# Expert jobs in pairs on TensorE, attention added by GpSimd, and a block closed without GpSimd's drain

## What is computed

```python
def _L0_attn_ref(x, W_off, b_off, W_attn, b_attn, W_out, b_out):
    off = (x @ W_off + b_off).reshape(Bx, Nx, H, P, 2)
    w = softmax((x @ W_attn + b_attn).reshape(Bx, Nx, H, P), axis=-1)
    idx = ...                                   # from off[..., 0], clipped to 0..127
    g = take_along_axis(x[:, 0, :], idx, axis=1)
    s = sum(g * w, axis=(2, 3))                 # one number per token
    return broadcast_to(s[..., None], (Bx, Nx, C)) @ W_out + b_out

def _ffn(x, w1, w2, w3):
    return silu(x @ w1.T) * (x @ w3.T) @ w2.T   # 128 -> 256 -> 128
# two shared experts for every token, and of 8 routed experts the best two per token,
# weighted by a softmax over their two logits
x = x + attn(xn) + ffn(xn)
```

## Time and profile before

| | |
|---|---|
| timed runs, median (range) | 418.75 us (418.43 to 419.17) |
| span of the profiled execution, first to last instruction | 416.8 us |
| busy: TensorE / VectorE / ScalarE / GpSimd | 366.9 (88%) / 331.8 (80%) / 190.5 (46%) / 189.7 (46%) us |
| mean granted TensorE clock | 0.985 of full speed |
| chain of work that ended last, by engine | PE 74%, DVE 13%, ACT 6%, DMA 2% |
| expert stage | 224.1 to 405.6 us |
| the shared experts' last sum ends | 224.95 us |
| the sums of the last job end | 406.46 us |

### The profile page before, as it was taken

One profiled execution on the slowest core, in us unless ns is written; L12 is line 12 of the kernel. 1 busy time (PEld: TensorE's weight loads), 2 busy tenths in 40 slices (PEclk: granted clock), 3 DMA queues, 4 the chain that ended last, 5 costly groups with the idle time before them and its releaser, 6 DMA issues.

```text
span 416.8 us, 12515 instructions
## 1 busy us (share of the span) xinstructions
PE 366.9 (88%) x4333; PEld 316.9 (76%) x4333; DVE 331.8 (80%) x929; ACT 190.5 (46%) x446; POOL 189.7 (46%) x152
## 2 busy tenths in 40 slices
PE   0157797789999999999999999999999999999990
PEld 0155564467677777777779999999999999999990
DVE  5988989987967699999996998886666666666760
ACT  2778728395322466666666344422222222222220
POOL 0434500404777776343200000001888888888863
PEclk9988999999999999999999999999999999999997
DMA  8944620000117199988873345554565956654332
GB/s 298 296 97 104 126 77 0 2 0 16 48 56 167 57 187 179 182 166 165 168 110 60 75 132 159 131 133 118 67 63 67 79 62 66 65 65 39 35 34 19
DMA packets 98871, 41.36 MB, mean 99 GB/s; under 512 B 73600, under 2 KB 92416, under 8 KB 98816
## 3 DMA queue, kind: packets, MB, share of 16 engines
q1 hardware_dynamic: 87120, 31.82, 36.7%
q0 software_dynamic: 11264, 8.69, 16.0%
q10 hardware_dynamic: 432, 0.11, 0.1%
HBM read 10.94 MB, written 12.88 MB: 57 GB/s over the span
## 4 chain that ended last, share of the span: by engine, by line
PE 74%; DVE 13%; ACT 6%; DMA 2%; issue 1%; POOL 1%; POOLq 0%; DVEq 0%; ACTq 0%
PE pY L832 18%; PE pY L655 11%; PE pAB L806 8%; PE pAB L804 8%; PE pAB L805 8%; PE pAB L643 5%; PE pAB L645 5%; PE pAB L644 5%; PE pV L667 4%; ACT units L870 3%; DVE hbuf L1189 2%; ACT wsp L941 2%; PE pV L621 2%; DVE hot L1095 1%; DMA xT<-hot 1%
## 5 line engine op out<-in xcount | busy, mean ns | idle before, releaser
L1065 POOL DMA_INDIRECT out_dram<-xT,rows x64 | 99.1, 1549 | 104.6 <-DMA out_dram<-base 83.3
L1011 ACT ACTIVATE units<-pAB 128x512 f32<-128x512 f32 x78 | 46.5, 596 | 119.6 <-PE pAB L806 119.6
L1053 POOL DMA_INDIRECT sorted_rows<-rows,slot x64 | 67.2, 1050 | 59.0 <-issue 32.3
L805 PE MATMUL pAB<-rows,wsp 128*128 128x128 f16 x512 | 89.0, 219 | 0.0
L806 PE MATMUL pAB<-rows,wsp 128*128 128x128 f16 x512 | 89.0, 219 | 0.0
L804 PE MATMUL pAB<-rows,wsp 128*128 128x128 f16 x512 | 89.0, 219 | 0.0
L832 PE MATMUL pY<-wsp,hbuf 128*128 (+1 forms) x620 | 86.4, 282 | 0.3 <-issue 0.3
L1476 DVE SCALAR_TENSOR_TENSOR hbuf<-pAB,units 128x512 f32<-128x512 f32 x78 | 53.6, 687 | 31.7 <-PE pAB L806 29.3
L832 PEld LDWEIGHTS pY<-wsp,hbuf 128*128 128x128 f32 x620 | 75.6, 192 | 0.8 <-issue 0.5
L655 PE MATMUL pY<-wsp,hbuf 128*128 128x128 f32 x512 | 70.2, 280 | 0.0
L655 PEld LDWEIGHTS pY<-wsp,hbuf 128*128 128x128 f32 x512 | 64.3, 192 | 4.1
(11 more groups left out here) (164 smaller groups left out, 586.1 us busy)
## 6 DMA issues: line engine op xcount, KB each, us to landing
base<-in_x SPq DMA_DIRECT2D x8, 512.0 KB, 7.5
out_dram<-base SPq DMA_DIRECT2D x16, 256.0 KB, 2.4
wraw<-in_wall SPq DMA_DIRECT2D x10, 256.0 KB, 2.8
rows<-hot SPq DMA_DIRECT2D x8, 256.0 KB, 2.7
proj<-sorted_rows SPq DMA_DIRECT2D x27, 68.5 KB, 1.9
wsp<-in_wall SPq DMA_DIRECT2D x10, 128.0 KB
sorted_rows<-rows,slot POOLq DMA_INDIRECT x64, 2.4
out_dram<-xT,rows POOLq DMA_INDIRECT x64, 3.4
```

The lines of the kernel that those rows point to most:

```text
L805: pe.matmul(o, hi, x(1), start=False, stop=False)
L1053: pool.indirect_dma_start(sorted_rows, bass.IndirectOffsetOnAxis(ap=slot[:, t:t + 1].bitcast(U32), axis=0), rows[:, t, :], None, bounds_ch ...
L1065: pool.indirect_dma_start(out_rows, bass.IndirectOffsetOnAxis(ap=meta[:, t, DEST - CW:DEST - CW + 1].bitcast(U32), axis=0), yt[:, t], None ...
```

## The change

1. `EXTRA_FROM` is 4: extras at places 4 to 17.
2. TensorE runs over pairs of jobs: turn of pair s, F of pair s-1, S of pair s-2, so F F S S instead of F S. The expert numbers are read five tiles ahead instead of three. VectorE makes its sums in pairs too, behind the product of the second job (`two_sums`).
3. The attention is added by GpSimd (`add_attention`), per block of four tiles a product into `attn_part` and a sum into `base`, before it waits for the writes and sends. SyncE writes block i once F(i) is done, from turn 8 on.
4. The side table is made at units 22 (VectorE), 25 (TensorE and ScalarE); `extra_table` behind unit 23. `sides` has a tile of its own, which `wp_raw` and `ident32` share.
5. The block is made with `no_gpsimd_drain=True`: GpSimd has no drain ahead of the closing barrier.

```diff
-SPREAD_UNIT = UNITS - 4
+SPREAD_UNIT, SIDES_UNIT = 22, 25
-ADDS = 3
-EXTRA_FROM = 8
+EXTRA_FROM = 4
...
-WRITE_AT = [min(n for n in range(AHEAD, STEPS) if FIRST_OF_TURN[n - AHEAD + 1] >= TPB * (i + 1) // ADDS + 5) for i in range(NB)]
+WRITE_AT = [min(n for n in range(AHEAD, STEPS) if LAST_OF_TURN[n - AHEAD] >= i) for i in range(NB)]
...
+        sides16 = sb("sides16", [P, TILES * 2 * E], F16)
+        wp_raw = sides16[:, 2 * P:2 * P + 2 * PROJ].bitcast(F32)
+        ident32 = sides16[:, 0:2 * P].bitcast(F32)
+        sides = sides16[:].rearrange("p (t k e) -> p t k e", k=2, e=E)
+        attn_part = aw_row[:, 0:2 * BLK].rearrange("p (r j c) -> p r j c", r=2, j=TPB)
...
-        block = ctx.enter_context(nc.Block())
+        block = ctx.enter_context(nc.Block(no_gpsimd_drain=True))
...
+                if n == SIDES_UNIT:
+                    pe.wait_ge(table_ready, 1)
+                    pe.wait_ge(spread_ready, 1)
+                    for b in range(2):
+                        mm = pe.matmul(pV[:, b, :], c["ones"][:], spread.rearrange("p t m -> p (t m)")[:, b * BLK:(b + 1) * BLK],
+                                       start=True, stop=True)
+                    mm.then_inc(sides_done, 1)
...
-                if q == 1:
-                    spread_sides()
...
-            pipeline(pe, NJOB, UNROLL, NJOB // UNROLL, [(0, r_turn), (SECOND, r_second), (FIRST, r_first)])
+            def of_pair(part):
+                def both_jobs(g, r):
+                    for q in (2 * (UNROLL * g + r), 2 * (UNROLL * g + r) + 1):
+                        part(q // UNROLL, q % UNROLL)
+                return both_jobs
+            pipeline(pe, NJOB // 2, UNROLL, NJOB // 2 // UNROLL, [(0, of_pair(r_turn)), (1, of_pair(r_first)), (2, of_pair(r_second))])
...
+            def add_attention():
+                for i in range(NB + 1):
+                    if i < NB:
+                        if i == 0:
+                            pool.wait_ge(attn_saved, APAIRS)
+                            pool.wait_ge(y_read, NB)
+                        if i >= 2:
+                            pool.wait_ge(attn_added, i - 1)
+                        nc.gpsimd.tensor_tensor(attn_part[:, i % 2], csum[:].unsqueeze(1).broadcast_to([P, TPB, P]),
+                                                attn_all[:, TPB * i:TPB * (i + 1)].unsqueeze(2).broadcast_to([P, TPB, P]),
+                                                ALU.mult).then_inc(attn_scaled, 1)
+                    if i:
+                        pool.wait_ge(attn_scaled, i)
+                        row = base[:, TPB * (i - 1):TPB * i, :]
+                        nc.gpsimd.tensor_tensor(row, row, attn_part[:, (i - 1) % 2], ALU.add).then_inc(attn_added, 1)
+            add_attention()
             pool.wait_ge(out_done, 16 * NB)
...
-            pipeline(dve, NJOB, UNROLL, NJOB // UNROLL, [(4, side_sums), (4, y_first), (4, y_second), (2, r_hf), (3, side_products),
-                                                         (3, r_attention), (4, load_tiles), (2, extra_shares)])
+            def two_sums(g, r):
+                if r % 2:
+                    for part in (side_sums, y_first, y_second):
+                        part(g, r - 1)
+                    for part in (side_sums, y_first, y_second):
+                        part(g, r)
+            pipeline(dve, NJOB, UNROLL, NJOB // UNROLL, [(2, r_hf), (4, two_sums), (3, side_products),
+                                                         (4, load_tiles), (2, extra_shares)])
```

More of the change, by code:

```diff
@@ L620, in routing_products @@
                     for a in range(NPAIR):
-                        mm = pe.matmul(pV[:, 1, 256:256 + NT], ident32[:], place[:, a, :], start=(a == 0), stop=(a == NPAIR - 1))
+                        mm = pe.matmul(pV[:, 1, 256:256 + NT], ident32, place[:, a, :], start=(a == 0), stop=(a == NPAIR - 1))
                     mm.then_inc(place_done, 1)
@@ L747, in first_addresses @@
                 elif u < 4:
-                    for k in range(2):
-                        ready_expert(u - 1, k)
+                    for t in {1: (0, 1), 2: (2, 3), 3: (4,)}[u]:
+                        for k in range(2):
+                            ready_expert(t, k)
                 else:
@@ L755, in _ @@
             straight(UNITS - ROUND, UNITS, both + [(0, first_addresses, UNITS - ROUND, UNITS)])
[L756 to L763, removed]
             def r_turn(g, r):
@@ L1412, in routed_low @@
                     split_low(g - (ATT - 1), u // 4)
-            while unit[0] < ROUND * ATT - 8:
-                shared_unit()
-            assert unit[0] == ROUND * ATT - 8
-            for n in range(8):
-                shared_unit()
-                one_hot(ATT - 1 + (n + 4) // ROUND, (n + 4) % ROUND)
-                if n >= 6:
-                    weighted_high(ATT - 1, n)
             def extra_table():
@@ L1434, in extra_table, with spread_out @@
                 v.scalar_tensor_tensor(active[:], f(0), 0.0, f(1), ALU.is_gt, ALU.mult).then_inc(extras_ready, 1)
-            def spread_out(g, u):
-                if ROUND * g + u == SPREAD_UNIT:
-                    for r in range(TURNS):
-                        dve.wait_ge(hot_turned[r], 16 * (BATCH - 1))
-                    v.tensor_tensor(spread, c["ident"][:, 0:TILES].unsqueeze(2).broadcast_to([P, TILES, 2 * E]),
-                                    tab_f[:, 2:2 + 2 * E].unsqueeze(1).broadcast_to([P, TILES, 2 * E]),
-                                    ALU.mult).then_inc(spread_ready, 1)
+            def spread_out():
+                dve.wait_ge(table_done, 1)
+                v.tensor_tensor(spread, c["ident"][:, 0:TILES].unsqueeze(2).broadcast_to([P, TILES, 2 * E]),
+                                tab_f[:, 2:2 + 2 * E].unsqueeze(1).broadcast_to([P, TILES, 2 * E]),
+                                ALU.mult).then_inc(spread_ready, 1)
+            while unit[0] < SPREAD_UNIT:
+                shared_unit()
+            spread_out()
+            while unit[0] < ROUND * ATT - 8:
+                shared_unit()
+            extra_table()
+            assert unit[0] == ROUND * ATT - 8
+            for n in range(8):
+                shared_unit()
+                one_hot(ATT - 1 + (n + 4) // ROUND, (n + 4) % ROUND)
+                if n >= 6:
+                    weighted_high(ATT - 1, n)
             start, end = ROUND * ATT, UNITS
@@ L1450, in _ @@
             rounds(dve, ATT + 1, UNITS // ROUND - 1, both)
[L1451 removed]
+            straight(UNITS - ROUND, UNITS + 4, both)
             extra_tile = {}
```

41 lines of the change are left out of this document (12 added, 29 removed).

## The result

| | before | changed |
|---|---|---|
| median of the runs timed together | 418.90 us (418.43 to 419.17, 4 runs) | 415.81 us (414.32 to 416.09, 4 runs) |
| ratio, 95% interval | | 0.992 (0.990 to 0.994) |
| profiled execution, span | 416.8 us | 412.5 us (the one of 414.32) |
| granted TensorE clock | 0.985 | 0.976 |
| GpSimd busy | 189.7 us | 225.3 us |

(The 418.75 ahead is the median of three of these four runs.) The change is faster by 3.1 us. In the two profiled executions it is 4.3. The changed kernel's executions differ among themselves: the four runs have spans of 412.5, 413.5, 413.9 and 414.3, and the profile is of the shortest. What a longer run has that this one hasn't is the main question of the experiments.

What follows compares the result with a forecast made beforehand. TensorE was taken to bound the expert stage, with a serial end of sums, sends and close. -0.3 (pairs, nearly eaten at the end) and -4.1 (no drain) made -4.4 us: span 412.4, median 414.4 us, range 413.2 to 418.8.

Steps and rivals of the forecast that it cites:

- the forecast's own case: The prediction's main case for the whole kernel: 414.4 us, bounds 413.4 to 415.6, chance 58%.
- the 416.6 of two rivals: GpSimd's attention slower than taken, or VectorE mildly delayed by the port (12%); or no gain from pairs on TensorE (5%).
- No drain, -4.1: Close of the block: without GpSimd's drain the wait after the last send shrinks, -4.1 us, bounds 4.4 saved and 0.
- The rival that the drain hides nothing: Close of the block: the 4.5 us wait is the barrier's or DMA queue's own; 418.5 us, chance 15%.
- Pairs on TensorE, -2.2: Expert stage: 39 fewer entries from first products (F) to float32 second products (S), 0.0557 us each, -2.2 us.
- +0.3 for S(76): Last jobs on TensorE: job 76's second products wait for the sums of job 74, +0.3 us, bounds 0.1 to 0.6.
- The end, "-0.3 in all": Last sends on GpSimd: four in a row nearly eat the pairs' gain, leaving -0.3 us, bounds -0.5 and +0.5.
- Side table, 0: Shared experts: the moved table delays VectorE's unit 24 product to about 119.4, hidden from TensorE; 0, bounds 0 and +0.5.
- Attention on GpSimd, 0: Expert stage: 2.35 us per block on an idle GpSimd, sixteen blocks to about 265; VectorE not the bound, 0.
- neither rival of it: VectorE waits for GpSimd at the shared SBUF port: severe 420.5 us, 8%; mild 416.6, 12% together with slower GpSimd.
- writes and loads, "5 us spare: 0": SyncE's queue: the last extra lands by 251.5, TensorE wants it at 256.5, so no cost.
- the distance of 1.95: Gap from the profiled span 416.8 to the median 418.75, kept to turn the predicted span 412.4 into 414.4 us.

Runs made afterwards that it cites:

- the execution that stalled: Profiled execution of the changed kernel run once more with nothing edited; span 413.4 us, median of its runs 415.16 us, ratio 0.9921 to the kernel before.

## Why the prediction held, and where it was off

**Direction and range** held: 415.81 lies in 413.2 to 418.8. The forecast of 414.4 was 1.4 too low, and the time lies just above the 413.4 to 415.6 given for the forecast's own case, nearer to the 416.6 of two rivals. The time alone would not tell these cases apart; the traces and the edits do.

**No drain, -4.1.** Right in mechanism and 0.3 too small: alone it is 4.4 in one group and 4.0 in another, 4.45 and 4.35 by the spans, and the wait at the close went from 4.5 to 0.2. The rival that the drain hides nothing is refuted from both sides.

**Pairs on TensorE, -2.2, with +0.3 for S(76).** Held. A step of two jobs went from 4.573 to 4.52, 0.053 x 39 = 2.05; with the wait of S(76) 1.82 was left at the last sum, where 1.9 was forecast. The price is paid per entry.

**The end, "-0.3 in all".** Right in mechanism, off by 0.4 within its bounds: +0.13. The delay from sum 74 to its send was 1.56 (401.54 to 403.10), the upper of the two values that I had read; I had taken 0.9.

**Side table, 0.** Held: 119.47 for 119.4. On TensorE its matmuls only changed places: with the clock at 1.00 from 25 to 50 us the first F comes at 224.15 (no pairs) instead of 223.76 (before, no drain), and from there to the last sum it is 181.67 instead of 182.05.

**Attention on GpSimd, 0.** Held. The product takes 1.04 and the sum 1.27, so 2.35 per block with the gaps, as forecast, and block 8 was done at 247.4 for 247.3. The last block was done at 262.7; the prediction's "about 265" was a slip, since 224.95 and 16 x 2.35 make 262.6. The Trainium skill (GPSIMD Engine Reference, section 3.1, Elementwise) led to an estimate of 1.12 us for such an operation; the two measured durations lie around it.

**The port.** It delays VectorE (L1533, 353 ns for 152), but neither rival of it came: behind the first pair of extras the pairs stay at 4.97 on TensorE. It was nearer than that sounds. The wait per job of extras was 0.61 us in the first profile and 0.73 in the second, where I had found 0.57 to fit and expected VectorE to be late from 0.75 on. The rule of the Trainium skill (SBUF — State Buffer, "Who interferes with whom") describes it rightly; the price was nothing, since two such waits, 1.2 to 1.5 us, just fit into the 1.5 of room per pair.

**The step that failed is that on writes and loads, "5 us spare: 0".** I followed the last extra's load, which the writes delay, and found it in time. It was in time, but with less to spare: issued at 252.59 instead of 249.6, landed by 255.3 even if it took the longest 2.7, asked for at 256.77:

```profile
252.59 0.33 SPq L530 DMA_DIRECT2D proj<-sorted_rows  x1
...
256.77 0.50 PE L779 MATMUL pV<-c_ident,proj 128*128 128x128 f16 x6
```

I wrote down that the loads now begin at about 221, and that TensorE transposes from job 4 on, but never set the first against the other. The first four extras are wanted together at 224.1 + 2 x 1.34 = 226.8, since the pair asks for both jobs. Their loads start at 221.8 or later, four at 0.83 and some 2 to land: 226.2 to 226.9 by the medians, 227.7 in the execution that stalled. The margin is nil, and the executions fall on both sides of it. Before, the extras were at place 8 and each job asked alone. The rows for this sum were there, but they would have given a margin of 1.2, not of nothing: 221, three times 0.89 and 1.9 make 225.6. The rest is that the first load started 0.8 to 2.1 later than the 221 that I took (221.81 to 223.10 in the five profiles), and that single loads take up to 2.7. So the sum would have pointed at the place, and not have given the size.

**From the span to the median.** I carried the distance of 1.95 over from the kernel before. Of the changed kernel each run lies 1.8 to 2.4 above its own span; but the profile is of one run, and here of the shortest. Its agreement with the forecast (412.5 for 412.4) was in part luck: it had no stall, and the 0.3 by which the drain was worth more and the 0.4 by which the end cost more nearly cancel.

**What stays open**: how the +1.3 us of the changed kernel with its drain restored divide. The profiled run of that kernel adds up by itself: its span is 0.9 above the profile of before, because the stage begins 1.10 later (225.16), is 2.20 shorter from there to the last sum (179.85 for 182.05), has 2.10 more to the last send and 0.1 less behind it. It had no stall, and its granted clock was 0.73 between 25 and 50 us, where before had 0.86. Some 0.4 of the 1.10 and of the 2.20 are the side table's, which changed places. The other runs of it would have to add the stall, 0.9 to 1.0 in some of them, and how often each of the two comes is not on record.

## To carry to other kernels

When a load is moved earlier in a queue, check the first use as well as the last; and when two jobs are joined to a pair, check the loads of both against the start of the pair. A gain on the engine that bounds the steady part reaches the end only if the serial tail, here sends of 1.85 each, does not get its work in a bunch: batch in the middle and go one by one at the end. And a profile of one execution can miss a stall that others have, here three of five: look at the spread of the runs before believing the margin.

## What the hardware showed that I had not expected

- GpSimd's drain at the close of the block cost 4.4 us, and 4.0 in another group (1.0% of this kernel): from the last send's start to the end of the span 8.3 and 8.2 us in the two kernels that have it, 3.8 to 4.0 in those that don't.
- The same kernel began its expert stage at 224.13 or 226.00, 1.9 us apart, and in the windows that I read the two differ by the granted clock: 0.50 in both from 30 to 35 us (the lower of its two levels, 1.2 GHz, after TensorE had been busy 1.85 and 2.30 us of the five before), then 0.99 and 1.00 in one (2.4 GHz), 0.72, 0.69 and, from 75 to 80, 0.66 in the other (mixtures of the two levels; before the last of them TensorE had been busy 2.36 us of five, and 2.49 in the execution that kept its clock; but the first profile of the changed kernel fell to 0.66 there too, behind the same 2.49). From 75 to 80 us the full clock gives 33 matmuls in 4.60 us of busy time, 0.66 gives 23 in 4.87.
- A VectorE operation of 128x1 with both inputs in SBUF, 154 ns alone, had a mean of 353 ns in one execution and 430 in another beside a GpSimd that did 128x512 operations without pause; a pair of them took 0.24 in some places and 1.22 in others.
